# Where the value product of the probabilities' low parts stands in the item, and when the next head's weights are split

## What is computed

```
q = rope(rmsnorm(x @ Wq.T));  k = rope(rmsnorm(x @ Wk.T));  v = x @ Wv.T
scores = q . [cached keys, k] * SCALE, masked
probs = softmax(scores)
o = probs @ [cached values, v];  out = o @ Wo.T
```

## Time and profile before

| what | value |
|---|---|
| median of 3 runs | 1282.56 us (1281.14 to 1286.61) |
| the profiled execution | 1286.0 us, span 1284.2 us |
| mean granted TensorE clock | 0.978 |
| busy: PE, PEld, DVE, ACT, POOL | 1193.3, 1003.8, 973.6, 848.6, 968.9 us |

### The profile page before, as it was taken

The page is one execution under the profiler, slowest core; times in us unless marked ns, Lnnn a source line. Parts: engine busy times, 40 slices in busy tenths (PEclk is TensorE's granted clock), DMA queues, the critical chain, the costliest instruction groups (busy, mean ns, idle before and its releaser), DMA issues.

```text
span 1284.2 us, 23898 instructions
## 1 busy us (share of the span) xinstructions
PE 1193.3 (93%) x6856; PEld 1003.8 (78%) x6856; DVE 973.6 (76%) x2388; ACT 848.6 (66%) x2441; POOL 968.9 (75%) x723
## 2 busy tenths in 40 slices
PE   6799997699999999998999999989998999999988
PEld 4577775578888878787888778878887888788778
DVE  3477856568787878787878788877887788778876
ACT  2677776566767667676766676667676777666741
POOL 1656656487888798888887988798879877987862
PEclk9899998999999999999999999999999999999999
DMA  7556554256665666566656565656665666556651
GB/s 262 199 186 235 217 219 153 68 120 157 143 141 134 154 142 145 121 151 138 140 127 147 130 159 120 158 128 145 148 158 120 142 146 141 132 131 135 152 148 66
DMA packets 336036, 191.32 MB, mean 149 GB/s; under 512 B 149153, under 2 KB 320162, under 8 KB 334882
## 3 DMA queue, kind: packets, MB, share of 16 engines
q1 hardware_dynamic: 334896, 189.63, 58.2%
q10 hardware_dynamic: 1010, 0.17, 0.1%
HBM read 101.66 MB, written 37.75 MB: 109 GB/s over the span
## 4 chain that ended last, share of the span: by engine, by line
PE 57%; POOL 22%; DMA 6%; issue 5%; ACT 4%; DVE 3%; SPq 3%; DVEq 0%; POOLq 0%; ACTq 0%
PE ps L1290 10%; PE ps L1292 10%; PE ps L1291 10%; POOL b_p_l L1731 9%; DMA b_moved<-b_blk_first 5%; PE ps L1358 4%; POOL b_w_l L1689 3%; SPq L1254 3%; PE ps L1351 3%; PE ps L1350 3%; PE ps L247 3%; ACT b_p_h L1493 2%; PE ps L1318 2%; PE ps L259 2%; PE ps L306 2%
## 5 line engine op out<-in xcount | busy, mean ns | idle before, releaser
L1731 POOL TENSOR_TENSOR b_p_l<-b_moved,b_p_h 128x1280 fp32r<-128x1280 f32 x128 | 379.1, 2962 | 86.9 <-ACT b_p_h L1493 86.9
L1591 DVE CUSTOM_DVE_ANT_0 b_sm<-ps,mask_row,b_rstd 128x640 f32<-128x640 f32 x256 | 223.0, 871 | 54.1 <-PE ps L1292 53.4
L1487 ACT ACTIVATE b_sm<-b_sm,b_mn 128x640 f32<-128x640 f32 x256 | 212.2, 829 | 76.3 <-DVE b_mn L1591 69.7
L1493 ACT ACTIVATE b_p_h<-b_moved 128x1280 fp32r<-128x1280 f32 x128 | 163.4, 1276 | 86.0 <-DMA b_moved<-b_blk_first 82.5
L1620 DVE SCALAR_TENSOR_TENSOR b_hacc<-ps,b_ri,b_hacc 128x512 f32<-128x512 f32 x248 | 182.7, 737 | 5.2 <-PE ps L1292 4.8
L1290 PE MATMUL ps<-b_w_h,x1t_h 128*128 128x512 f32 (+1 forms) x512 | 184.1, 360 | 1.0 <-DVE b_qt_l L1578 0.8
L1291 PE MATMUL ps<-b_w_l,x1t_h 128*128 128x512 f32 (+1 forms) x512 | 178.1, 348 | 0.0
L1292 PE MATMUL ps<-b_w_h,x1t_l 128*128 128x512 f32 (+1 forms) x512 | 177.1, 346 | 0.0
L1290 PE MATMUL ps<-b_kt_h,b_qt_h 128*128 128x320 f32 x512 | 163.4, 319 | 1.5 <-DVE b_mn L1591 1.5
L1291 PE MATMUL ps<-b_kt_l,b_qt_h 128*128 128x320 f32 x512 | 158.2, 309 | 0.0
L1292 PE MATMUL ps<-b_kt_h,b_qt_l 128*128 128x320 f32 x512 | 157.8, 308 | 0.0
(11 more groups left out here) (174 smaller groups left out, 3175.9 us busy)
## 6 DMA issues: line engine op xcount, KB each, us to landing
b_moved<-b_blk_first SPq DMA_DIRECT2D x256, 160.0 KB, 3.3
b_moved<-b_blk_second SPq DMA_DIRECT2D x256, 160.0 KB, 3.1
kv_of_batch<-in_kv SPq DMA_DIRECT2D x128, 256.0 KB
b_ck<-kv_of_batch SPq DMA_DIRECT2D x64, 256.0 KB, 4.3
b_cv<-kv_of_batch SPq DMA_DIRECT2D x256, 64.0 KB, 2.6
raw<-in_w SPq DMA_DIRECT2D x32, 384.0 KB, 4.8
raw<-in_wo SPq DMA_DIRECT2D x32, 256.0 KB, 4.2
a_xt<-in_xt SPq DMA_DIRECT2D x8, 256.0 KB, 6.3
```

Source lines behind the costliest of these rows:

```text
L1487: act.activation(sm[:, h % 2], sm[:, h % 2], ACT.Exp, bias=mn[:, m.b % 2, h:h + 1], scale=-1.0, accum_out=rs[:, m.b % 2, h:h + 1]).then_in ...
L1493: act.activation(pair_of(p_h, pair), moved_pair(pair), ACT.Copy).then_inc(mh_sb, 1)
L1591: dve.tensor_tensor_reduce(sm[:, h % 2], score_row(h), mask_row[:, m.b], rstd[:, m.b % 4, h:h + 1], -MASKED, ALU.add, ALU.min, mn[:, m.b % ...
L1731: pool.tensor_tensor(pair_of(p_l, pair), moved_pair(pair), pair_of(p_h, pair), ALU.subtract).then_inc(ml_sb, 1)
```

## The change

TensorE: `values_of_lows(last)` moves behind `project_q(two)`; `project_kv(two)` and `scores(one, 0)` now stand ahead of `out(last, 0)` and `out(last, 1)`. The output products' banks are exchanged (`OT, SM, OT, SM`). GpSimd: the sum for the rotated keys (`key_sum`) goes ahead of `low_probs(last, 1)`; the sum for the rotated queries (`rope_queries`) goes ahead of `low_probs(m, 0)`; all four query weights are done in slot 5 and all four output weights in slot 1; `low_probs(m, 0)` of slot 5 is put off to slot 6. ScalarE, VectorE and the weight loads on SyncE follow. No instruction is added or removed.

```diff
@@ -1119,7 +1119,7 @@
         sem = lambda n: ctx.enter_context(nc.semaphore("b_" + n))
         (sync_first, tensor_first, scalar_first, vector_first, gpsimd_first), (xl_sb, x1_out) = first_stage
         SC, OT, SM, PJQ, PJK = (0, 2), 4, 5, 6, 7
-        OUT = (SM, OT, OT, SM)
+        OUT = (OT, SM, OT, SM)
         NK = NT * P
         CUT = NK // 2
         LEAD = 512 - CUT
@@ -1258,8 +1258,8 @@
                 blocks_across(m, 1)
                 if two:
                     key_rows(two)
-                if m.b in (2, 3, 4, 5):
-                    chunk(m.g + 1, m.b - 2)
+                if m.b in (1, 2, 3, 4):
+                    chunk(m.g + 1, m.b - 1)
                 if m.b in (6, 7) and m.g + 1 < G:
                     chunk(m.g + 1, KT + m.b - 6)
                 if m.b == 0 and m.g > 0:
@@ -1367,8 +1367,8 @@
                     wait(pe, h_sb, REP * m.n)
                 if m.b == 0:
                     pe.wait_ge(wol_sb, KT * m.g + h + 1)
-                if h == 2:
-                    pe.wait_ge(h_sb, REP * m.n + 2)
+                if h > 1:
+                    pe.wait_ge(h_sb, REP * m.n + h - 1)
                 tile = slice(h * P, (h + 1) * P)
                 three(ps[:, OUT[h], :], (o_h[:, tile], o_l[:, tile]), (wo_h[:, h], wo_l[:, h])).then_inc(wo_ps, 1)
 
@@ -1386,22 +1386,23 @@
                 scores(m, 3)
                 if last:
                     values_of_highs(last)
-                    values_of_lows(last)
                 if one:
                     turn_new(one)
                 if two:
                     project_q(two)
+                if last:
+                    values_of_lows(last)
                 if m.n == end.n:
                     gate_rows(pe, 0)
                 if m.n == end.n - 1:
                     turn_rows(pe, 0)
+                if two:
+                    project_kv(two)
+                if one:
+                    scores(one, 0)
                 if last:
                     out(last, 0)
                     out(last, 1)
-                if one:
-                    scores(one, 0)
-                if two:
-                    project_kv(two)
                 if m.n == end.n - 1:
                     turn_rows(pe, 1)
                 if m.n == end.n:
@@ -1441,12 +1442,13 @@
                 wait(act, wo_ps, REP * (B * g - 1) + c + 1)
                 act.activation(wo_h[:, c], raw[:, c, 0:D], ACT.Copy).then_inc(woh_sb, 1)
 
-            def squares(m):
+            def squares(m, heads=range(REP)):
                 act.wait_ge(qab_sb, m.n + 1)
                 wait(act, rstd_sb, m.n)
-                for h in range(REP):
+                for h in heads:
                     op = act.activation(squares_out[:, h], ps[:, PJQ, h * P:(h + 1) * P], ACT.Square, accum_out=ss[:, h:h + 1])
-                op.then_inc(qsq_sb, 1)
+                if h == REP - 1:
+                    op.then_inc(qsq_sb, 1)
 
             def new_kv(m):
 
@@ -1511,38 +1513,39 @@
                     h_out(act, 1)
                 if one:
                     queries(one)
+                    cache_keys(one)
+                if m.b == 1:
+                    out_weights(m.g, 0)
+                    out_weights(m.g, 1)
+                exponent(m, 2)
+                if one:
+                    turned_key(one)
                 if m.b == 6:
-                    q_weights(m.g + 1, 2)
-                    q_weights(m.g + 1, 3)
-                if one:
-                    cache_keys(one)
+                    kv_weights(m.g + 1)
+                exponent(m, 3)
                 if m.b == 1:
                     out_weights(m.g, 2)
                     out_weights(m.g, 3)
-                exponent(m, 2)
-                if m.b == 6:
-                    kv_weights(m.g + 1)
                 if one:
-                    turned_key(one)
-                exponent(m, 3)
-                if last:
-                    output(last)
-                if one:
+                    cache_values(one)
                     new_keys(one)
-                    cache_values(one)
-                high(m, 0)
-                if m.n == end.n - 1:
-                    h_out(act, 0)
-                if two:
-                    squares(two)
-                if m.b == 0:
-                    out_weights(m.g, 0)
-                    out_weights(m.g, 1)
                 if m.b == 5:
                     q_weights(m.g + 1, 0)
                     q_weights(m.g + 1, 1)
+                if last:
+                    output(last)
+                if m.b == 5:
+                    q_weights(m.g + 1, 2)
+                    q_weights(m.g + 1, 3)
+                if m.n == end.n - 1:
+                    h_out(act, 0)
+                high(m, 0)
+                if two:
+                    squares(two, range(REP - 1))
                 if one:
                     exponent(one, 0)
+                if two:
+                    squares(two, range(REP - 1, REP))
 
             scalar_first(act, (q_weights, kv_weights, squares, new_kv, queries, turned_key, cache_keys, new_keys, cache_values))
             slots(act, slot)
@@ -1624,6 +1627,8 @@
 
             def slot(m, one, two, last):
                 before = last.before() if last else None
+                if before:
+                    accumulate(before, 1)
                 turn_blocks(m, 0)
                 minima(m, 1)
                 if before:
@@ -1632,18 +1637,15 @@
                     new_values(one)
                 minima(m, 2)
                 turn_blocks(m, 1)
+                if one:
+                    queries(one)
                 if before:
                     accumulate(before, 3)
                 if m.n == end.n:
                     h_rest(dve, 1)
                 minima(m, 3)
-                if one:
-                    queries(one)
                 turn_blocks(m, 2)
                 turn_blocks(m, 3)
-                if last:
-                    output(last)
-                    invert(last)
                 if one:
                     new_keys(one)
                 if m.n == end.n - 1:
@@ -1651,11 +1653,12 @@
                 if two:
                     rope_products(two)
                 if last:
-                    accumulate(last, 0)
+                    output(last)
+                    invert(last)
                 if one:
                     minima(one, 0)
                 if last:
-                    accumulate(last, 1)
+                    accumulate(last, 0)
 
             def low_weights(g, c):
 
@@ -1670,6 +1673,7 @@
 
             vector_first(dve, (rope_products, new_values, queries, new_keys, minima, low_weights, low_kv_weights))
             slots(dve, slot)
+            accumulate(end.before(), 1)
             accumulate(end.before(), 2)
             accumulate(end.before(), 3)
             choose(dve, 0)
@@ -1733,29 +1737,30 @@
             def slot(m, one, two, last):
                 if one:
                     rms(one)
+                    key_sum(one)
+                if m.b == 6:
+                    low_probs(last, 0)
                 if last:
                     low_probs(last, 1)
-                if one:
-                    key_sum(one)
                 if m.b == 6:
-                    q_weights(m.g + 1, range(2, KT))
+                    kv_weights(m.g + 1)
                 if one:
                     cache_keys(one)
                 if m.b == 1:
+                    out_weights(m.g, 0)
+                    out_weights(m.g, 1)
                     out_weights(m.g, 2)
                     out_weights(m.g, 3)
-                if m.b == 6:
-                    kv_weights(m.g + 1)
                 if one:
                     cache_values(one)
-                low_probs(m, 0)
+                if m.b == 5:
+                    q_weights(m.g + 1, range(2))
                 if two:
                     rope_queries(two)
-                if m.b == 0:
-                    out_weights(m.g, 0)
-                    out_weights(m.g, 1)
                 if m.b == 5:
-                    q_weights(m.g + 1, range(2))
+                    q_weights(m.g + 1, range(2, KT))
+                else:
+                    low_probs(m, 0)
 
             pool.memset(half[:], -0.5).then_inc(const_sb, 1)
             pool.wait_ge(const_sb, 1)
```

## The result

The changed kernel takes **1343.95 us** (median of 4 runs, 1340.31 to 1344.23) against 1283.75 us for the kernel before on the same chips: ratio 1.046, interval 1.043 to 1.049. The forecast was 1247 us and faster; it is 60 us slower. The profiled execution has a span of 1338.5 us.

The account below looks back on a forecast made before the run. TensorE bounds ordinary items; only a 58 us loop excess can be won. Remaining 25 (slot 6 14.0 + 0.7, slots 1 and 2 1.2, clock 4, unassigned 5), gain 33 plus 2 to 3: 1282.6 - 36 = 1247 us, range 1234 to 1268.

Parts of the forecast that it names:

- step 1: Low products behind the query projection get 2.9 us more; the output's cover shrinks to 2.3 but holds, 1.4 an item otherwise.
- rival C: Slot 6 costs 4 us a group as GpSimd's pile starts 2 us later, slow stretch each time: 1267 us, chance 0.14.
- step 3: GpSimd's query sum ahead of `low_probs(m, 0)`: `b_ra` ready 4 us ahead of the next `turn_q`, removing 9.4 us of waits.
- Step 2: New keys' transpose 1.17 us earlier, key sum moved ahead too: cost 0; ScalarE's 94.8 us wait for `b_kb` mostly goes.
- Rival F: Slower: the new keys' transpose (`turn_new`) waits 0.7 to 0.8 us in every item; 1293 us, chance 0.06.
- Step 4: Slots 1 and 2: no low-product stall in slot 1; `b_ka` slightly late in slot 2, about 0.15 us where 2.2 was lost.
- Step 5: Slot 6: low products stall 0.7 us, key and value projection 1.2, in 7 groups; the last group only 0.7.
- a start after a wait: Restart of TensorE's weight loads after its stalls on low products: about 0.17 us each, 2.5 in total.
- two or three were said: Slow clock stretches remaining for the seven double pauses in slot 6: 1.5 us each, about 4 us.
- The 5 us left unassigned: Part of TensorE's 58 us loop excess given no cause; the forecast kept it as remaining after the change.
- Step 6: Banks, VectorE order and chunk loads one slot earlier: cost 0; a few tenths per item if the cover went.
- a slow stretch behind every pair of pauses: Slot 6's seven double pauses each followed by a slow clock stretch: 10.5 us, 6.5 more than the forecast took.

Follow-up runs that it names:

- third buffer: The changed kernel with all its orders plus a third buffer for the high part of the cached values: 1247.69 us, 0.972 of the kernel before.
- low products alone: The kernel before with one edit, the low products moved behind the query projection: 1433.00 us, 1.116 of before.
- GpSimd's order alone: The kernel before with two GpSimd exchanges: key sum ahead of the second low pair, query sum ahead of the first. 1310.30 us, 1.022 of before.
- key copy first: The changed kernel with ScalarE's new-keys copy back ahead of its cached-values copy: 1277.85 us, 0.9956 of the kernel before.
- the projection last in the slot: The changed kernel with the key and value projection back behind first scores and output products: 1384.80 us, 1.080 of the kernel before.
- slot 6 reordered, on top of the third buffer: Third buffer kernel; slot 6: GpSimd's cached keys before key/value weights, TensorE's scores and outputs before key/value projection; last group's low probabilities not put off: 1241.31 us.
- output copy ahead of the values' copy: Key copy first, plus ScalarE's cached-values copy behind the output copy and GpSimd's values subtraction behind the query sum: 1261.86 us, 0.982 of before.
- low products back: The changed kernel with the low products back behind the high ones, all else as changed: 1339.01 us, 1.044 of the kernel before.

## Why the prediction was wrong

- **The step that failed** is step 1. It lists what follows the low products as "the copy and rest of the output" and prices that cover. But the low products also free a half of the values' buffer, and the copy that wants this half stands on ScalarE ahead of the new keys' copy in the changed order; no step takes up that exchange. Step 1 gave the copy no wait, and steps 4 and 5 took the cached values' subtraction as ready whenever GpSimd came to it. Where the prediction has nothing, there stands a wait of 1.27 us in each item: 78.3 us in the table, some 94 with what each start after a pause costs. The third buffer takes away just this, and the time is 1247.69 where 1247 was said; the changed kernel is 96 us above that.
- With the pair in its old order, the same oversight still costs 30 us, from 1248 to 1278. Somewhat over half of these are the late pile of GpSimd and the late output copy; the other 13 or so, an estimate from the lengths of the items in slot 6, are the clock, which fell in seven groups instead of one. That is the picture of rival C (a later pile, and a slow stretch each time), for another reason than rival C gives. In the changed kernel, whose items are longer, this part is mostly hidden: the low products wait 1.3 us in slot 6, and the output's low part is not waited for in slot 5.
- Step 1's price of the output's cover, 1.4 an item if it is gone, was right (1.41 longest, 87.0 us in 63 times, in the run with the low products alone). So was step 3: no wait for `b_ra` in any run with the new order and the low products in their new place.
- Step 2: "cost 0" held in ordinary items, and ScalarE's wait for `b_kb` fell from 94.8 to 0.3 us. Rival F had the right form (something waits in every item behind a changed order, 36/61 = 0.6 us decides), and the wrong wait. I looked for it at `turn_new` because its slack was in the rows. The one that came, with its restart, was 1.54.
- Step 4: no low product waits in slots 1 and 2: right. The transpose of the new keys comes 0.24 us late in slot 1, where nothing was said, and 0.19 in slot 2, where 0.15 was said: some 3 us in all instead of 1.2 (run with the third buffer).
- Step 5, in the same run: 0.7 and 1.0 us where 0.7 and 1.2 were said, in 7 groups. Wrong there: the last group, where no query projection covers the low products, waited 3.4, not 0.7.
- The rest of the sum: a start after a wait was priced at 0.17 us and cost 0.27. The clock fell in one of seven groups, where two or three were said, but again, for eight us, behind the last group's pause. The 5 us left unassigned went as well. These errors of a few us cancelled, so that the agreement to 1 us is partly luck.
- Step 6, "cost 0": the banks and VectorE's order caused no wait that I found, but no run tried them alone. That stays open, and so does the loads' move by one slot.

## What to carry to other kernels

When work is moved later on one engine, list everything that its end releases: not only who reads its result, but who waits to overwrite its inputs. The semaphore waits of the code give this list; the trace of before does not, since a wait that is always met in time leaves no row. Then look at what is queued behind each such waiter on its engine. Orders of several engines can serve one another, and one of them alone can then be worse than none: here GpSimd's order alone cost 26 us and the low products' move alone 149. Such orders are tested together, or the resource that couples them (here the buffer) is doubled.

## What the hardware showed

How often the granted clock falls behind a pause of TensorE differs with the pause here. Windows of four us (columns as in the earlier trace rows) from the run with the key copy first, with pauses of 1.78 and 1.00 us between 838 and 844:

```profile
836.00:840.00 4.00, 3.73 (x17) 2.65 (x15) 3.76 (x8) 2.37 (x6) 4.00 (x2) 1.00 0.01 3
840.00:844.00 4.00, 1.49 (x6) 0.96 (x6) 1.07 (x2) 0.96 (x2) 4.00 (x3) 0.88 0.86 193
844.00:848.00 4.00, 4.00 (x18) 4.00 (x19) 0.78 (x2) 2.19 (x8) 4.00 (x4) 0.50 1.04 209
```

and from the run with the third buffer, with pauses of 0.67 and 1.00 us in the same place of the program:

```profile
699.00:703.00 4.00, 4.00 (x18) 2.88 (x16) 3.61 (x7) 2.86 (x7) 4.00 (x2) 1.00 0.17 28
703.00:707.00 4.00, 2.33 (x14) 1.80 (x14) 2.06 (x4) 1.14 (x2) 4.00 (x3) 1.00 0.89 201
707.00:711.00 4.00, 4.00 (x27) 3.69 (x26) 2.12 (x4) 2.78 (x13) 4.00 (x4) 1.00 0.99 224
```

In the first the engine runs four us at 0.50, the lower level (1.2 GHz); in the second it stays at 2.4. These are one group each. Counted over the loop of each profiled execution, from windows of one us:

| run | pauses of TensorE, us | followed by a stretch at the lower level |
|---|---|---|
| the changed kernel, ordinary items | 1.27 alone | 0 of 54 |
| the projection last in the slot, ordinary items | 1.5 and 0.5 | 0 of 53 |
| slot 6 reordered, on top of the third buffer | 0.7 and 0.4 | 0 of 7 |
| third buffer | 0.7 and 1.0 | 1 of 7 |
| before, slots 1 and 6 | 1.9 to 2.2 alone | 6 of 15 |
| the changed kernel, slot 6 | 1.3 and 1.3 | 3 of 7 |
| output copy ahead of the values' copy | 1.6 and 1.0 | 3 of 7 |
| key copy first | 1.8 and 1.0 (or 0.3) | 7 of 7 |
| low products back | about 4.0 alone | 8 of 8 |

In slot 6 the clock fell more often the longer the idle time was, but the length alone does not settle it: 1.5 and 0.5 us in ordinary items were never followed by a slow stretch, and pauses of about 2.6 us were followed by a slow stretch in 14 of 14 cases in the run with the low products alone and in 6 of 14 in the run with GpSimd's order alone. The 62 pauses of 1.27 us, one every 16 us, left the changed kernel's mean clock at 0.983, where the kernel before had 0.978.

The Trainium skill's page "TensorE: Matmul & The Clock Gate", section "A second HAM failure mode: psum-queue depth-cycling", by which frequent short idles can make the clock swing, made me weigh a slow stretch behind every pair of pauses. For the pair forecast, 0.7 and 1.0 us, this did not come (1 of 7); for the pair of 1.8 and 1.0 it did (7 of 7).
